# VectorE's order in a two-layer attention and expert kernel: both numerator banks divided at the start of the next step, and experts marked two heads later in the second layer

## The reference, cut to what matters

```python
x = x + jnp.tanh(g_xattn[0]) * _L0_xattn_ref(_layernorm(x), ctx_1024, ctx_1024, ...)   # causal mask, 16 heads
x = x + jnp.tanh(g_ffn[0]) * _L0_ffn_ref(_layernorm(x), ...)        # shared expert + top 2 of 8, hidden 256
x = x + jnp.tanh(g_xattn[1]) * _L1_xattn_ref(_layernorm(x), ctx_1024, ctx_1024, mask_B_ik0, ...)  # mask by length
x = x + jnp.tanh(g_ffn[1]) * _L1_ffn_ref(_layernorm(x), ...)        # top 2 of 8, hidden 1024
# attention: probs = softmax(scores); out = einsum(probs, vh); out.reshape(...) @ Wo.T
# experts: topk_w, topk_i = top_k(scores, 2); comb = (one_hot(topk_i, 8) * topk_w[..., None]).sum(1)
```

## Time and profile before

| what | us |
|---|---|
| median of 3 runs | 1748.24 (1747.21 to 1750.28) |
| the profiled execution, its own time | 1747.6 |
| span in the profile, first to last instruction | 1745.9 |
| busy in the span: PE, weight loads, DVE, ACT, POOL | 1392.2, 1176.9, 1112.2, 793.0, 727.3 |
| first and last numerator transposition (L888) | 91.3, 1277.8 |

### The profile page before, as it was taken

How to read it: one execution, slowest core, us unless ns; L and a number is a source line. 1 busy time by engine, 2 the same in 40 slices (tenths; PEclk the granted TensorE clock), 3 DMA queues, 4 the chain that set the end, 5 groups by cost and what they waited for, 6 DMA issues and landing times. The chain is left out here.

```text
span 1745.9 us, 39897 instructions
## 1 busy us (share of the span) xinstructions
PE 1392.2 (80%) x12001; PEld 1176.9 (67%) x12002; DVE 1112.2 (64%) x3589; ACT 793.0 (45%) x1744; POOL 727.3 (42%) x630
## 2 busy tenths in 40 slices
PE   3798988888872777735888887878736999999997
PEld 3576767677651677734556555655426999999997
DVE  4588787877663455523788888887645555555543
ACT  2354545555430555532455455554422544544543
POOL 4334444444231366643344444443232344445422
PEclk9899999999985899975899999999977999999998
DMA  2333334333216677651333333332263324334322
GB/s 88 100 97 100 103 93 110 100 98 88 80 44 185 130 122 131 103 98 55 102 106 102 110 99 109 99 106 65 66 181 105 89 45 96 90 90 96 91 42 42
DMA packets 213629, 168.26 MB, mean 96 GB/s; under 512 B 21462, under 2 KB 207096, under 8 KB 213240
## 3 DMA queue, kind: packets, MB, share of 16 engines
q1 hardware_dynamic: 181112, 126.05, 26.3%
q0 software_dynamic: 26880, 35.80, 12.1%
q10 hardware_dynamic: 5504, 4.75, 1.0%
HBM read 63.80 MB, written 51.56 MB: 66 GB/s over the span
## 5 line engine op out<-in xcount | busy, mean ns | idle before, releaser
L1806 POOL DMA_INDIRECT out_rows<-e_y,e_token x68 | 110.5, 1625 | 235.6 <-DVE e_y L1862 215.8
L1888 ACT ACTIVATE e_h<-e_h,t_up_bias 128x256 f32<-128x256 f32 x272 | 110.5, 444 | 209.0 <-PE e_h L1924 209.0
L938 DVE TENSOR_REDUCE a_row_max<-a_scores 128x2 f32<-128x512 f32 x256 | 170.7, 680 | 41.5 <-PE a_scores L1579 39.9
L1268 ACT ACTIVATE s_w_rows<-a_scores_t 128x384 f32<-128x384 f32 (+1 forms) x256 | 137.7, 547 | 109.9 <-PE a_scores_t L1597 59.9
L1268 ACT ACTIVATE a_probs<-a_scores_t 128x384 f32<-128x384 f32 (+1 forms) x256 | 136.0, 546 | 108.0 <-PE a_scores_t L1597 58.3
L771 POOL DMA_INDIRECT routed_rows_dram<-r_rows,r_slot x128 | 128.3, 1003 | 94.0 <-issue 60.5
L1939 PE MATMUL e_y_bank<-e_down_hi,e_hidden_hi 128*128 128x256 f32 x544 | 157.9, 290 | 3.2 <-DVE e_hidden_lo L1835 3.2
L1924 PE MATMUL e_h<-e_xs_hi,e_up_hi 128*128 128x256 f32 x544 | 154.6, 284 | 3.7 <-DVE e_xs_lo L1827 3.5
L2097 POOL DMA_INDIRECT x_mid_dram<-l_y,l_token x76 | 119.0, 1565 | 86.7 <-ACT l_token L2191 48.5
L1924 PE MATMUL e_h<-e_xs_lo,e_up_hi 128*128 128x256 f32 x544 | 153.8, 283 | 0.0
L1939 PE MATMUL e_y_bank<-s_k_stack,e_hidden_hi 128*128 128x256 f32 x544 | 153.6, 282 | 0.0
(11 more groups left out here) (288 smaller groups left out, 4450.3 us busy)
## 6 DMA issues: line engine op xcount, KB each, us to landing
s_q_stack<-a_parts SPq DMA_DIRECT2D x384, 64.0 KB
s_k_stack<-a_parts SPq DMA_DIRECT2D x384, 64.0 KB
l_xs_rows<-routed_rows_dram SPq DMA_DIRECT2D x42, 258.0 KB
e_xs_rows<-routed_rows_dram SPq DMA_DIRECT2D x36, 258.0 KB
a_ctx_rows<-in_ctx SPq DMA_DIRECT2D x32, 256.0 KB, 3.2
t_up<-in_L_ffn_W SPq DMA_DIRECT2D x8, 1024.0 KB
t_down<-in_L_ffn_W SPq DMA_DIRECT2D x8, 1024.0 KB
routed_rows_dram<-pad_rows ACTq DMA_DIRECT2D x16, 258.0 KB, 9.9
```

Source lines behind the costliest of these rows:

```text
L938: nc.vector.reduce_max(row_max[:, :, h], bank[:].rearrange("p (c t) -> p c t", c=TC), AX_X).then_inc(maxed, 1)
L1268: nc.scalar.activation(probs[h % NP][:, 0:width], scores_t[h % 2][:, 0:width], ACT.Exp).then_inc(probs_ready, 1)
L1806: pool.indirect_dma_start(out=x_acc, out_offset=bass.IndirectOffsetOnAxis(ap=token[p][:, c:c + 1], axis=0), in_=y[p][:, c, :], in_offset=N ...
L1888: nc.scalar.activation(out, h_bank[g][:, at:at + TS], act_func, bias=routed.up_bias[:, bass.ds(e * FC + fc, 1)]).then_inc(hidden_ready, 1)
```

## The change

DVE divides bank 0 of an item no longer at heads 14 and 15 of the item's own step, but at the start of the next one, ahead of bank 1. Bank 1 is transposed right behind it, and its reciprocal and multiplication move from there to behind the maxima of head 1, its transposition back to behind those of head 2. In the second layer `index_to_float` and `mark_chosen` move from head 6 to head 8; in the first layer they stay at head 5. One constant line is added, so lines below L566 have numbers one higher.

```diff
+        MARK_AT = 5 if soft else 8
...
             def step(i):
                 if i.has(-1):
+                    turn_heads(i, -1, 0)
+                    scale_heads(i, -1, 0)
+                    turn_back(i, -1, 0)
                     turn_heads(i, -1, 1)
-                    scale_heads(i, -1, 1)
-                    turn_back(i, -1, 1)
...
                     if i.has(1):
                         row_maxima(i, h)
+                    if h == 1 and i.has(-1):
+                        scale_heads(i, -1, 1)
+                    if h == 2 and i.has(-1):
+                        turn_back(i, -1, 1)
...
-                    if h == GATE_AT + 4 and i.has(-2):
+                    if h == MARK_AT and i.has(-2):
                         index_to_float(i)
...
-                    if h == GATE_AT + 4 and i.has(-2):
+                    if h == MARK_AT and i.has(-2):
                         mark_chosen(i)
...
-                    if h == 14 and i.has(0):
-                        turn_heads(i, 0, 0)
                     if h == 14 and i.has(4):
                         ln_apply(i.at(4), i.par(4))
-                    if h == 15 and i.has(0):
-                        scale_heads(i, 0, 0)
-                        turn_back(i, 0, 0)
```

## The result

| | median us | lowest to highest | runs |
|---|---|---|---|
| before | 1749.68 | 1746.98 to 1757.08 | 20 |
| changed | 1754.33 | 1747.87 to 1766.11 | 20 |

The ratio is 1.0032, with a 95% interval of 1.0019 to 1.0046: the changed kernel is 0.3% slower. The forecast was 1717, with a range of 1694 to 1742. The profiled execution took 1756.4 us, 2.1 above its median; its span is 1754.7 against 1745.9. The page of the changed kernel: span, TensorE's busy time, and the row of its granted clock in 40 slices of the span, in tenths.

What follows compares the result with a forecast made beforehand. No engine was taken as full in the attention phases; waits, with DVE setting the pace, bounded the step. Gains of 11 + 14 + 8, less 2 for the last steps, made 31 us off 1747.6: 1717 as a median, range 1694 to 1742.

Steps and rivals of the forecast that it cites:

- the cast at 0.16 us: Second layer, DVE's cast of expert indices: expected back at about 0.17 us, from 1473 ns on average.
- PE's gap ahead of `turn_max_late`: PE's idle at the step border, 1.36 us in the first layer, 1.72 in the second; expected near 0 in both.
- R3: Rival, chance 0.10: POOL comes first with L779 at every second-layer border, delaying the multiplication behind head 1; slower, 1759 us.
- Part A: Second layer, marking two heads later: 0.9 us a step gained, 11 us in all, bounds 6 and 19.7.
- Part B: First layer's border, division work removed ahead of `add_shared`: 14 us gained, bounds 10 and 19.
- If the scatter sets them, they move as the scatter does: First layer's border: if scatters set when PE's results arrive, arrivals come 0.6 us earlier, the low end of the gain.
- the lag: First-layer border: PE's scores ended 2.2 us before DVE took them, against 0.04 us in an early step without scatters.
- The row of the 2.46 us wait: First layer, start of step: DVE's 2.46 us idle, where the four moved instructions were to run before the scores arrive.
- Part C: Second layer's border, division work moved: net 0.5 us a border, 8 us gained in all, bounds -20 and 30.
- R1: Rival, chance 0.17: PE alone sets all arrivals at both layers' borders; 50 us gained, 1698 us.
- R2: Rival, chance 0.18: scatters set the arrivals at the borders and the locks cost; 12 us gained, 1736 us.
- R4: Rival, chance 0.05: nothing moves, DVE's saved time becomes waiting for PE and marks collide elsewhere; 1748 us.

Runs made afterwards that it cites:

- g1_after: The changed kernel run again on chip E, beside the kernel before: ratio 1.0021.
- g4_marks: The kernel before with only the marks moved from head 6 to head 8 in the second layer, on chip E: ratio 0.9965 to the kernel before.
- h2_warm14: The changed kernel plus 14 idle matmuls behind head 1 in first-layer steps, on chip F: ratio 0.9936 to the kernel before.
- h3_after: The changed kernel run again on chip F, beside the kernel before: ratio 1.0023.
- e1_marks: The kernel before with only the marks moved to head 8 in the second layer, on chip B: ratio 0.9950 to the kernel before.
- f1_after_first1: The changed kernel with the first layer's four scatters moved behind the next step's first subtraction, on chip D: ratio 0.9778 to the kernel before.

## Why the prediction was wrong

**Right, on every chip:** the cast at 0.16 us, PE's gap ahead of `turn_max_late` gone in both layers, bank 1's multiplication at 0.42 us on average in the second layer. R3, the way to a slower kernel that I gave 0.10, did not happen: L780 grew from 2.12 to 2.36 us on average over ten steps, DVE was first, POOL waited. That was luck as much as judgement, since at eight of thirteen borders DVE's multiplication started only 0.02 us ahead of L780. By the Trainium skill (SBUF — State Buffer, Who interferes with whom) the earlier instruction makes the other wait, and the trace agrees with these numbers. (The prediction tied the cast to the case of two SBUF inputs, but a cast reads one; that it stood still beside L790 is in the rows all the same.)

**Part A, the marks, was somewhat over-sized:** 11 us forecast, 8.1 measured alone on chip B and 6.8 on chip E. Beside the divisions on chip B it was the forecast 0.9 us a step.

**Part B, the first layer's border, is the step that failed.** I bounded its gain by 10 us from below, from "If the scatter sets them, they move as the scatter does". That took one reading of the lag for a fixed distance. Behind the first scatter's start the key projection of the kernel before ends 3.6 us, that of the changed kernel 2.7 us. In the kernel before the landing was at 4.5 us or at 6.0 us, in turn on chip A, which makes its steps of 28.0 and 30.2 us, and in no fixed order on chips C and E. In the changed kernel it is always at 5.9 to 6.3. The work ended 0.9 us nearer to the scatters' start and still missed the earlier landing every time; why, no run shows. The row of the 2.46 us wait was the sign, and the neighbouring steps, 28.0 and 30.2 us long in turn, would have shown that the lag was no constant. Measured with g1_after beside g4_marks on chip E, which differ in the divisions alone: 14 us forecast for this border, 7.4 lost between the first and the sixteenth query projection; on chip A 8.3.

**The clock was no term at all.** Taking away the short gap of 1.36 us ahead of `turn_max_late` left one long gap instead of two short ones, behind which the clock falls at every border. The falls cost at least 1.4 us a step of the changed kernel, by h2_warm14 against h3_after. Part of that the kernel before paid already: it was slow for 3.4 us at every second border, 1.7 a step, against mostly 6.8. My estimate from these rows is that three quarters, about 1.0 us a step, are new. By the Trainium skill (TensorE: Matmul & The Clock Gate, Part 1: The HAM clock gate) the clock follows how busy TensorE has been recently, and the trace agrees: it fell behind idle pieces. The term could have been asked for beforehand, since the trace of the kernel before has six stretches at 0.50 between 140 and 460 us.

**Part C, the second layer's border:** 8 forecast, with bounds -20 and 30. With g1_after and g4_marks on one chip, twelve steps from the fourth query projection on took 331.1 and 327.1 us: 4 lost. The reason I priced, locks between POOL and DVE, was not it; the counts were.

**R1, "all arrivals are PE's", 50 us,** is nearly what chip B did: 40 us for the divisions, and for the marks 8.1 alone or, beside the divisions, 12 steps of 0.9. Its total is added up from these, as the changed kernel was not run there. R2 had the right cause on the other chips, and its 1736 us was off by 18, by the wrong bound in part B and the clock. R4's number, 1748, lay nearest; DVE's saved time did turn into waiting, as it said, but for late counts and not for PE's work, and the marks collided with nothing. "PE's gap goes and the first maxima are no earlier" was named as what would show me wrong, and did; so was a step of 28 us or longer in the second layer, and it was 28.1.

What stays open is why these chips differ, and what holds the counts up: POOL's making of the transfers or their traffic. No run took one without the other. By the Trainium skill (DMA: Bandwidth & Descriptors, Latency and other measured facts) the descriptor rings of DMAs that GpSimd issues lie in SBUF behind ports that two of the sixteen DMA engines use as well, and contention at these ports is its uncertain guess for why those two are slower. It says nothing of counts, and no run here shows that this is the cause.

## What to carry to other kernels

When the trace shows a count that lands late, plot its lateness over many steps against what runs beside it before pricing any work that ends there; a lag that alternates is no constant. An idle gap taken off TensorE only to reappear as one longer wait can cost in clock as much as it saved (here at least 1.4 us a step), so ask where the gap goes. Spread POOL's indirect transfers instead of issuing four at a step's border, and time such a change on several chips: here the same divisions were worth -2.3% on one chip and +0.7% on another.

## What the runs showed of the hardware that was not expected

- Everywhere but on chip B, PE's counts land late while POOL's four indirect DMAs run (4.8 to 5.1 us in the first layer), and recorded landings come in bunches: stretches of 0.5 to 1.6 us in which the trace has no landing at all, up to about 6 us behind the first one's start. With two of them at the border the last such stretch ended at the median 3.0 us behind it. At the borders of the first layer the kernel before on chip A had four to six such stretches, e1_marks on chip B at most one. In f1_after_first1 they moved with the scatters, away from the border.
- These stretches rest in part on records that are missing: the trace of the kernel before on chip A holds 23024 updates of counts, that of e1_marks on chip B, which makes the same ones, 27042. The lateness does not rest on them, since DVE and ACT start that late, in the first-layer border above 3.1 us behind PE's scores. Whether the missing records and the late counts have one cause is open.
- The same kernel took 1700.6 us on chip B and 1745 to 1756 on the others.
- In the first layer TensorE's granted clock fell to 0.50 for 3.4 us at every second border of the kernel before, which has idle pieces of 1.36 and of up to 1.5 us there, and for mostly 6.8 us at every border of the changed kernel, whose idle piece is 1.9 to 2.4 us. With 14 idle matmuls in that piece it stayed at 1.00 over nearly all borders (one fall between 160 and 430 us in h2_warm14).
